# Routing a tile later and its row marks in two operations, expert blocks written out, expert sums in pairs of tiles

## The chip, the core and the metric

The kernel runs on one core of a Trainium2 chip. The metric is the device time of one execution in microseconds (us), as the median over runs; less is better. The five engines are named as in the profile: PE (matrix products; PEld is its weight load), DVE (vector), ACT (scalar activations), POOL (GpSimd, here mostly transfers by index) and SP (which starts the other transfers).

## What is computed

The input is 1024 rows (16 sequences of 64) of 256 numbers. Four layers are added to it in turn, each on a layer norm of the rows: an attention over a context, a mixture of eight experts, a second attention with rotated queries, and a second mixture of 32 masked experts of which each row takes one. The change touches the first mixture and what lies next to it:

```python
x = x + attention_0(layernorm(x), ctx, ctx)
# the first mixture, on h = layernorm(x):
logits = h @ router_w.T
top_w, top_i = top_k(softmax(logits), 2)            # two experts for each row
top_w = top_w / sum(top_w)
for e in range(8):
    gate, up = bitlinear(h, gate_w[e]), bitlinear(h, up_w[e])
    y_e = bitlinear(up * square(relu(gate)), down_w[e])
    out = out + combine[:, e:e + 1] * y_e
x = x + out
x = x + attention_1(layernorm(x), ctx, ...)
x = x + masked_experts(layernorm(x), ...)
# bitlinear(x, w) = quantised rows (scale 127 / max|row|) @ ternary weights (-1, 0, 1, times a mean).T
```

## The kernel before

The 1024 rows lie as eight tiles of 128 rows. Each engine has its own instruction stream, written out in order by hand, and the streams meet in semaphores.

**The first attention** goes over the eight tiles t. In the same passes ACT and DVE make the eight experts' weights ternary. DVE adds each tile's attention to X (`add_att`), measures the tile's mean and variance and hands it to POOL, which subtracts the mean (XC). At the pass t = 5 DVE also centres the router's weights (`r_raw`, three operations that wait for each other); at t = 7 PE turns them and ACT copies them to `rT`, in the middle of the tile's work. After the last tile DVE takes the largest value of each row (`row_peaks`), and PE makes the router's logits.

**Routing** places 2048 pairs of row and expert into 23 blocks (`NBLK`) of 128 rows, each block of one expert. `positions` works out the place of each pair and then marks, for each of 16 groups c of 128 pairs, the row of the block in a 128x128 table (`at_row`, 16 operations on DVE). PE's `sort` multiplies these marks with two tables for each group (which tile, which row of the tile): 32 matmuls into one sum, from which `owners` reads, with one conversion, which row of X belongs to each place of each block. POOL fetches the rows of a block by that list (`indirect_dma_start`, x_rows to xg).

**The expert blocks j = 0..22.** For each block: PE turns the fetched rows (`turn_rows`, L822), ACT copies them (L1311), PE makes gate and up (`gate_up`, L840), ACT makes relu (L1319), DVE multiplies relu by gate (L1747, below: gated) and by up (L1751), takes the largest magnitude of each row (L1755), from it the scales (L1726 to L1734, one number for each row), and the hidden rows are scaled and rounded: for even blocks by DVE (L1738), for odd blocks by ACT (L1333). PE turns the hidden rows (`turn_hidden`, L851), ACT copies them (L1323), PE makes the product with the third weight (`down`, L858), ACT scales the result (L1329), and POOL stores it by index (L602). In step j PE does `turn_hidden(j)`, `turn_rows(j+4)`, `gate_up(j+3)` and `down(j)` in this order. PE and DVE hold blocks 0 to 3 written out, then a loop of four blocks that is run `ROUNDS` = 4 times (on PE), and the rest written out; ACT's stream is written out. The expert of a block is read from a register that `run_of` loads, once for a turn of the loop, as seven experts in one word.

**Around the end of the blocks** PE folds the next attention's weights, eight units u (`fold_queries`, `fold_values`, `fold_keys`); units 0 and 1 are woven into the last three blocks. SP waits for the last stored block and loads the experts' results back (yg, four pairs of tiles). DVE adds them: for each tile two operations (L1824, L1825), each waiting for the one before, then the measure (L1840); after tiles 3 and 7 means and variances, POOL takes the roots, DVE makes the normed rows XN (L1818), PE turns them (L1060), ACT and DVE split them, and `project` (L981) starts the second attention. From there to the end PE's products set the pace.

Of the kernel before, what the change touches and what calls it, by code (L numbers as in the profile page):

```python
# [9 lines left out]
P = 128  # L10
NT = 8
# [101 lines left out]
def build(nc, x, ctx_in, cst_in, sel_in, kv_in, router_w, ffn_w, fold_in,  # L113
          weight_t, scale, masks_t, router_dt, out):
    with ExitStack() as ctx:
# [41 lines left out]
        iota_b = sb("iota_b", [P, P], BF16)  # L157
# [193 lines left out]
        raw_used, w_summed, w_total, w_rec_ready, hid_acted = (sem(n) for n in ("raw_used", "w_summed", "w_total", "w_rec_ready", "hid_acted"))  # L351
# [11 lines left out]
        h_scale_ready, relu_ready = sem("h_scale_ready"), sem("relu_ready")  # L363
# [51 lines left out]
        def positions(dve, link, R, start):  # L415
# [18 lines left out]
        def owners(dve, R, nth, B):  # L434
# [21 lines left out]
        def sort(pe, R, B, nth):  # L456

            n = R.choices * NT
            for c in range(n):
# [93 lines left out]
        def _(pool):  # L553
# [16 lines left out]
            pool.tensor_scalar(iota_b[:], cst[:, C_IOTA:C_IOTA + P], 1.0, 0.0, ALU.mult, ALU.add).then_inc(bconsts_built, 1)  # L570
# [77 lines left out]
        def _(pe):  # L648
# [115 lines left out]
            for t in range(NT):  # L764
# [9 lines left out]
                if t == NT - 1:  # L774
                    pe.wait_ge(r_centred, 1)
                    pe.wait_ge(w_rec_ready, NT)
                    for k in range(2):
                        mm = pe.transpose(bank[7][:, R_TURNED + k * NE:R_TURNED + (k + 1) * NE], r_raw[:, k * P:(k + 1) * P],
                                          identf[0:NE, 0:NE])
                    mm.then_inc(r_turned, 1)  # L780
# [8 lines left out]
                turn_probs(t, 3)  # L789
            turn_x1(2)  # L790
# [26 lines left out]
            def turn_rows(j, q, r):  # L817

                pe.wait_ge(gathered[r], 16 * q + 16)
# [12 lines left out]
            def in_run(word, k):  # L832
# [1290 lines left out]
```

## Time and profile before

| | us |
|---|---|
| median of 3 runs (444.98 to 446.79) | 445.58 |
| the profiled execution | 447.06 |
| its span, first to last instruction | 444.9 |
| PE busy | 371.3 |
| DVE busy | 329.6 |
| ACT busy | 212.3 |
| POOL busy | 142.9 |

The profiled execution is 1.5 us above the median of the runs; 2.2 us of it lie outside the span. Busy times are summed over the whole span, whose stages have different limits, so they don't say what a change in one stage is worth. The granted TensorE clock is a mean of 0.941 of full speed.

### The profile page before, as it was taken

Reading aid. Unit: us, or ns where it says so; the run is one execution under the profiler, and the core shown is the slowest. Engines: PE = TensorE matmul, PEld = TensorE weight load, DVE = VectorE, ACT = ScalarE, POOL = GpSimd, SP = SyncE. Lnnn points to the kernel's source line nnn. Section 1 sums busy time; section 2 is a strip of 40 time slices with the busy share of each in tenths; the row PEclk is TensorE's granted clock in tenths of the full one; section 3 lists DMA queues with packets and bytes.
Section 4 is the critical chain, followed back from the end, with each engine's and each line's share of the span. In section 5 each row is a group of like instructions: output and inputs, shape, how many; then the busy total and the mean of one; then the engine's idle time right before and its main releaser. Section 6 shows DMA issues by size and latency. Waiting matters only on the chain.

```text
span 444.9 us, 10555 instructions
## 1 busy us (share of the span) xinstructions
PE 371.3 (83%) x3670; PEld 257.3 (58%) x3677; DVE 329.6 (74%) x847; ACT 212.3 (48%) x466; POOL 142.9 (32%) x147
## 2 busy tenths in 40 slices
PE   2687877935877779989999999999999989538995
PEld 1466666922444446767457566466574778526884
DVE  6959999797888887798588778886875544673453
ACT  3699998552778887763013222231232221225441
POOL 1111211325466644020283142240440410153334
PEclk9999998955799999998999999999999999859999
DMA  8996760421365531540103112022031101343001
GB/s 271 405 411 224 296 246 4 173 66 36 85 213 165 178 136 49 176 159 14 66 30 96 43 55 96 2 95 96 1 97 55 41 1 70 121 113 89 19 32 38
DMA packets 17199, 50.77 MB, mean 114 GB/s; under 512 B 2120, under 2 KB 6480, under 8 KB 15104
## 3 DMA queue, kind: packets, MB, share of 16 engines
q1 hardware_dynamic: 14288, 42.46, 26.7%
q0 software_dynamic: 2864, 7.68, 5.8%
q8 instruction: 30, 0.49, 0.5%
q14 instruction: 17, 0.14, 0.1%
HBM read 43.44 MB, written 6.69 MB: 113 GB/s over the span
## 4 chain that ended last, share of the span: by engine, by line
PE 60%; DVE 14%; ACT 10%; issue 7%; DMA 6%; SPq 1%; POOL 1%; ACTq 0%; DVEq 0%; POOLq 0%
PE bank L981 17%; PE bank L1195 8%; PE bank L997 6%; PE bank L1069 5%; DMA raw<-in_L_ffn_w_dram 3%; PE bank L840 3%; PE bank L1008 3%; PE bank L851 3%; ACT W L1228 2%; PE bank L1022 2%; PE bank L858 2%; ACT hid L1333 2%; PE bank L1048 2%; PE bank L1032 2%; PE bank L710 1%
## 5 line engine op out<-in xcount | busy, mean ns | idle before, releaser
L1799 DVE TENSOR_TENSOR roped<-bank,cst 128x512 f32<-128x512 f32 x96 | 61.1, 685 | 29.4 <-PE bank L981 28.4
L623 POOL TENSOR_TENSOR WE<-WE,wT 128x512 f32<-128x512 f32 x32 | 42.3, 1348 | 82.0 <-DMA WE<-_L_ffn_expert_masks_dram 82.0
L981 PE MATMUL bank<-XNT_hi,AW_hi 128*128 128x512 f32 x96 | 42.2, 439 | 0.0
L1378 ACT ACTIVATE qrT<-bank 128x512 f32<-128x512 f32 x16 | 8.7, 595 | 62.3 <-PE bank L1008 62.3
L981 PE MATMUL bank<-XNT_lo,AW_hi 128*128 128x512 f32 x96 | 38.0, 396 | 0.0
L981 PE MATMUL bank<-XNT_hi,AW_lo 128*128 128x512 f32 x96 | 37.8, 394 | 0.0
L1372 ACT ACTIVATE prob<-prob 128x512 f32<-128x512 f32 x16 | 10.1, 632 | 44.3 <-DVE prob L1809 44.3
L997 PE MATMUL bank<-roped,MW 128*64 128x512 f32 x128 | 31.0, 605 | 0.0
L1069 PE MATMUL bank<-VW,ctxT 128*128 128x256 f32 x128 | 30.7, 385 | 0.0
L981 PEld LDWEIGHTS bank<-XNT_hi,AW_hi 128*128 128x128 f32 x96 | 18.2, 190 | 19.5 <-issue 11.4
L602 POOL DMA_INDIRECT y_rows<-y,slot x23 | 22.6, 983 | 20.7 <-ACT y L1329 18.3
L840 PE MATMUL bank<-W,xgT 128*128 x86 | 25.6, 423 | 3.0 <-ACT xgT L1311 2.6
L595 POOL DMA_INDIRECT xg<-x_rows,owner_b x23 | 22.4, 973 | 17.6 <-ACT hs L1314 11.0
L1228 ACT ACTIVATE W<-raw 128x1024 bf16<-128x1024 f32 x24 | 25.4, 1071 | 3.3 <-DMA raw<-in_L_ffn_w_dram 3.3
L576 POOL TENSOR_SCALAR XC<-X,mv 128x256 f32<-128x256 f32 x7 | 10.7, 1524 | 45.8 <-DVE mv L1620 45.8
L851 PE MATMUL bank<-identf,hid 128*128 128x128 f32 x92 | 15.3, 291 | 11.5 <-ACT hid L1333 7.1
L1069 PEld LDWEIGHTS bank<-VW,ctxT 128*128 128x128 f32 x128 | 23.2, 190 | 2.6
L710 PE MATMUL bank<-identf,pnat 128*128 128x128 f32 x128 | 21.8, 298 | 2.8 <-ACT pT L1220 2.8
L1747 DVE SCALAR_TENSOR_TENSOR hid<-bank,relu 128x512 f32<-128x512 f32 x23 | 15.9, 690 | 10.9 <-ACT relu L1319 10.8
L1195 PE MATMUL bank<-WE,pT_d 128*128 x80 | 21.4, 407 | 1.3 <-ACT pT_d L1457 0.7
L1500 DVE TENSOR_REDUCE mx<-bank 128x8 f32<-128x512 f32 x32 | 19.8, 681 | 1.9 <-PE bank L676 1.8
L1323 ACT ACTIVATE hidT<-bank,less_magic 128x512 bf16<-128x512 f32 x23 | 15.8, 687 | 10.7 <-PE bank L851 10.6
(313 smaller groups left out, 896.0 us busy)
## 6 DMA issues: line engine op xcount, KB each, us to landing
raw<-in_L_ffn_w_dram SPq DMA_DIRECT2D x8, 1536.0 KB, 8.1
fold<-in_L_xattn_fold_dram SPq DMA_DIRECT2D x8, 1024.0 KB, 6.6
WE<-_L_ffn_expert_masks_dram SPq DMA_DIRECT2D x8, 1024.0 KB, 5.3
kv<-in_keys_values_dram SPq DMA_DIRECT2D x8, 656.0 KB, 9.3
yg<-y_rows SPq DMA_DIRECT2D x8, 256.0 KB, 5.2
x_tok<-pay SPq DMA_DIRECT2D x8, 256.0 KB, 2.2
X<-in_x_dram SPq DMA_DIRECT2D x4, 256.0 KB, 10.1
x_rows<-xrow SPq DMA_DIRECT2D x2, 258.0 KB, 3.4
```

Source lines behind the costliest of these rows:

```text
L595: pool.indirect_dma_start(out=xg[j % 4][:].bitcast(U32), out_offset=None, in_=x_rows, in_offset=bass.IndirectOffsetOnAxis(ap=RB.owner[:, j ...
L602: pool.indirect_dma_start(out=y_rows, out_offset=bass.IndirectOffsetOnAxis(ap=slot[:, b:b + 1], axis=0), in_=y[b % 4][:], in_offset=None). ...
L623: pool.tensor_tensor(WE[:, e], WE[:, e], wT[:], ALU.mult).then_inc(WE_ready, 1)
L710: mm = pe.transpose(bank[4 + kvl % 2][:, c * P:(c + 1) * P], pnat[kvl][:, c * P:(c + 1) * P], identf[:])
L840: mm = pe.matmul(bank[2 + 2 * m - par][:], xgT[par][:, k * P:(k + 1) * P], W[:, bass.ds(e, 1), m, k * FF:(k + 1) * FF].rearrange("p a i -> ...
L851: mm = pe.transpose(bank[5][:, k * P:(k + 1) * P], hid[r][:, k * P:(k + 1) * P], identf[:])
L981: mm = pe.matmul(bank[g][:], a[:, k, c * P:(c + 1) * P], b[:, k, g * 512:(g + 1) * 512], start=k == 0 and i == 0, stop=k == 1 and i == 2)
L997: pe.matmul(bank[2 + g][half(h, g) * S:(half(h, g) + 1) * S, :], MW[u][:, r, at:at + S], roped[n][:, r, :], start=r == 0, stop=False, skip ...
L1069: mm = pe.matmul(bank[t % 4][:, 0:H], ctxT[:, u, t * P:(t + 1) * P], VW[:, u, :], start=u == 0, stop=u == NU - 1)
L1195: mm = pe.matmul(bank[4 + r % 4][:, 0:H], pT_d[r % 4][:, k * P:(k + 1) * P], WE_k[:, bass.ds(e, 1), k, :].rearrange("p a o -> p (a o)"), s ...
L1228: ins = act.activation(W[:, e, m, :], raw[e % 3][:, m, :], ACT.Abs, accum_out=w_sum[e % 2][:, m:m + 1])
L1799: ins = dve.tensor_tensor(roped[n][:, r, :].rearrange("p (b s) -> p b s", s=S), src, cst[:, None, at:at + S].to_broadcast([P, 8, S]), ALU. ...
```

## The change

Four parts:

1. The router's weights are centred at the pass t = 6 on DVE (was t = 5), turned by PE and copied by ACT after the passes (was in the middle of t = 7). `row_peaks` takes tiles 0 and 1 at t = 7, tile 2 later and 3 to 6 last (was 0, then 1, then 2 to 6).
2. The 16 marks become two operations of eight groups each. `sort` has one matmul of two tables (46 columns) for each group, and `owners` adds the two halves in two operations. POOL's `iota_b` goes.
3. The blocks are written out on PE and DVE. DVE scales every block's hidden rows, ACT none; ACT makes the output scale (one number for each row). `down` comes one step later: in step j PE does `turn_hidden(j)`, `turn_rows(j+4)`, `gate_up(j+3)` and `down(j-1)`; one `down` is left at the end. Two words of experts are loaded at the start, three more in steps 2, 6 and 10.
4. The experts' results are added in pairs of tiles, the first operation of both tiles ahead of the second of either. PE turns the first two pairs of XN after `fold_queries(7)` and ahead of `fold_values(7)` and `fold_keys(7)` (was after them).

```diff
@@ positions, owners (DVE), sort (PE)
-            dve.wait_ge(bconsts_built, 4)
-            for c in range(n):
-                dve.tensor_scalar(R.at_row[:, c], iota_b[:], lo[:, c:c + 1], None, ALU.is_equal).then_inc(spots_ready, 1)
+            for k in range(R.choices):
+                c = slice(k * NT, (k + 1) * NT)
+                dve.tensor_tensor(R.at_row[:, c], lo[:, c, None].to_broadcast([P, NT, P]),
+                                  cst[:, None, C_IOTA:C_IOTA + P].to_broadcast([P, NT, P]), ALU.is_equal).then_inc(spots_ready, 1)
...
-            dve.tensor_copy(R.owner[:], B[:, 0:R.n_blk]).then_inc(owner_ready, 1)
+            link(dve.tensor_copy(owner_tile[:], B[:, R.n_blk:2 * R.n_blk]))
+            dve.tensor_tensor(R.owner[:], owner_tile[:], B[:, 0:R.n_blk], ALU.add).then_inc(owner_ready, 1)
...
-                pe.wait_ge(spots_ready, c + 1)
-                for part in (1, 2):
-                    mm = pe.matmul(B[:, 0:R.n_blk], R.at_row[:, c, :], R.of_block[:, part, c, :],
-                                   start=c == 0 and part == 1, stop=c == n - 1 and part == 2)
+                pe.wait_ge(spots_ready, c // NT + 1)
+                mm = pe.matmul(B[:, 0:2 * R.n_blk].rearrange("p (a b) -> p a b", a=2), R.at_row[:, c, :], R.of_block[:, 1:3, c, :],
+                               start=c == 0, stop=c == n - 1)
@@ blocks, PE
-            with pe.Fori(0, ROUNDS) as i:
-                word = run_of(i)
-                for r in range(4):
-                    j = 4 * i + r
-                    e_up, e_down = in_run(word, r + 3), in_run(word, r)
-                    turn_hidden(r, 2 * i + r // 2)
-                    turn_rows(j + 4, i + 1, r)
-                    gate_up(j + 3, (r + 1) % 2, e_up)
-                    down(j, r % 2, e_down)
...
+            runs = [run_of(i) for i in range(2)]
+            for j in range(NBLK):
...
+                turn_hidden(j)
+                if j + 4 < NBLK:
+                    turn_rows(j + 4)
+                if j + 3 < NBLK:
+                    gate_up(j + 3, expert_at(j + 3))
+                if j:
+                    down(j - 1, expert_at(j - 1))
+                if j % 4 == 2 and len(runs) <= ROUNDS:
+                    runs.append(run_of(len(runs)))
...
+            down(NBLK - 1, expert_at(NBLK - 1))
...
             for u in range(2, NU):
                 fold_queries(u, 0)
                 fold_queries(u, 1)
+                if u == NU - 1:
...
+                    turn_x2(0)
+                    turn_x2(1)
                 fold_values(u)
                 fold_keys(u)
@@ blocks, ACT
-                if j % 2 == 0 and j + 1 < NBLK:
-                    scale_hidden(j + 1)
-                outputs(j)
+                output_scale(j)
+                if j:
+                    outputs(j - 1)
+            outputs(NBLK - 1)
@@ first attention, DVE
-                    row_peaks(0, 1)
+                    row_peaks(0, 2)
...
-                if t == NT - 3:
+                if t == NT - 2:
                     dve.wait_ge(r_loaded, 16)
...
-            row_peaks(2, NT - 1)
+            row_peaks(3, NT - 1)
@@ blocks, DVE (written out, one step)
+                if j:
+                    link.after(highest)
+                    scale = link.note(dve.tensor_scalar(was[:, 2:3], was[:, 1:2], was[:, 0:1], EPS, ALU.mult, ALU.max))
...
+                gated = link.note(dve.scalar_tensor_tensor(h[:], bank[2 - par][:], 0.0, relu[par][:], ALU.max, ALU.mult))
+                if j:
+                    link.after(scale)
+                    inverse = link.note(dve.reciprocal(was[:, 3:4], was[:, 2:3]))
+                link.after(gated)
+                dve.tensor_tensor(h[:], h[:], bank[4 - par][:], ALU.mult).then_inc(hid_done, 1)
+                if j:
+                    link.after(inverse)
+                    factor = link.note(dve.tensor_scalar(was[:, 4:5], was[:, 3:4], was[:, 0:1], QMAX, ALU.mult, ALU.mult))
+                dve.wait_ge(hid_done, j + 3)
+                highest = link.note(dve.tensor_reduce(hs[j % 4][:, 1:2], h[:], AX.X, ALU.max, apply_absolute_value=True))
+                if j:
+                    link.after(factor)
+                    dve.tensor_scalar(hid[(j - 1) % 4][:], hid[(j - 1) % 4][:], was[:, 4:5], MAGIC, ALU.mult, ALU.add).then_inc(hid_scaled, 1)
@@ sums, DVE
-            for t in range(NT):
-                add_experts(t)
-                link(dve.bn_stats(stats[:, t, :], X[:, t, :]))
-                if t == NT // 2 - 1:
-                    half_variances(0)
-            half_variances(1)
+            for c in range(NT // 2):
+                added = first_choices(c)
+                if c == 2:
+                    aggregated = half_means(0, measured)
+                second_choices(c, added)
+                if c == 2:
+                    half_variances(0, aggregated)
+                measured = measure(c)
+            half_variances(1, half_means(1, measured))
```

## Rows read from the trace of the kernel before

**Rows 1.** The page, the chain that ended last: shares of the span.

```profile
PE 60%; DVE 14%; ACT 10%; issue 7%; DMA 6%; SPq 1%; POOL 1%; ACTq 0%; DVEq 0%; POOLq 0%
```

**Rows 2.** Timeline, end of the first attention: start us, duration us, instruction [idle before <-releaser].

```profile
69.01 0.38 DVE L1623 BATCH_NORM_STATS2 r_stats<-r_raw 8x6 f32<-8x256 f32 x1
...
74.92 2.07 ACT L1214 ACTIVATE pnat<-bank 128x512 f32<-128x512 f32 x4 [0.44 <-PE bank L701]
...
79.64 0.36 DVE L1521 RECIPROCAL den_rec<-bank 128x32 f32<-128x32 f32 x1 [1.27 <-PE bank L732]
...
87.27 1.48 DVE L1515 TENSOR_REDUCE row_max<-XC 128x5 f32<-128x1280 f32 x1
```

**Rows 3.** Timeline, routing: marks, sort and owners.

```profile
95.92 3.28 DVE L432 TENSOR_SCALAR at_row_b<-iota_b,pos_b 128x128 bf16<-128x128 bf16 x16
...
97.09 2.40 PE L465 MATMUL bank<-of_block_b,at_row_b 128*128 128x23 bf16 x32 [4.32 <-DVE at_row_b L432]
...
99.52 0.18 DVE L437 CAST owner_b<-bank 128x23 uint32<-128x23 f32 x1
```

**Rows 4.** Tile at_row_d (second mixture): duration ns min/median/max, start.

```profile
L1949 DVE TENSOR_TENSOR at_row_d<-slot_lo,cst x1: 1219/1219/1219, 389.3 to 389.3; 128x1024 bf16<-128x1024 uint32 x1
```

**Rows 5.** Waits, 95 to 240 us: us in total, times, longest us.

```profile
DVE hid L1747 <- ACT relu L1319: 10.8, 17, 2.0
...
PE bank L851 <- ACT hid L1333: 7.1, 10, 0.8
...
PE bank L851 <- issue: 4.1, 4, 1.3
```

**Rows 6.** Timeline of PE: turn_hidden of blocks 1, 11 and 19.

```profile
117.07 0.66 PE L851 MATMUL bank<-identf,hid 128*128 128x128 f32 x4 [0.76 <-ACT hid L1333]
...
145.77 0.66 PE L851 MATMUL bank<-identf,hid 128*128 128x128 f32 x4 [0.69 <-ACT hid L1333]
...
168.75 0.65 PE L851 MATMUL bank<-identf,hid 128*128 128x128 f32 x4 [0.70 <-ACT hid L1333]
```

**Rows 7.** Timeline of DVE: block 13, and the next block's first operation.

```profile
145.08 0.68 DVE L1747 SCALAR_TENSOR_TENSOR hid<-bank,relu 128x512 f32<-128x512 f32 x1
...
145.80 0.68 DVE L1751 TENSOR_TENSOR hid<-hid,bank 128x512 f32<-128x512 f32 x1
...
146.72 0.68 DVE L1755 TENSOR_REDUCE hs<-hid 128x1 f32<-128x512 f32 x1
147.32 0.48 DVE L1738 TENSOR_SCALAR hid<-hid,hs 128x512 f32<-128x512 f32 x1
148.19 0.69 DVE L1747 SCALAR_TENSOR_TENSOR hid<-bank,relu 128x512 f32<-128x512 f32 x1 [0.40 <-ACT relu L1319]
```

**Rows 8.** Timeline of POOL in the blocks: one fetch.

```profile
145.15 0.97 POOL L595 DMA_INDIRECT xg<-x_rows,owner_b  x1 [0.31 <-issue]
```

**Rows 9.** Line L830, PE's register load of a word: ns min/median/max.

```profile
L830 PEldq TENSOR_LOAD <-run_e x5: 300/427/495, 111.0 to 159.6; - x5
```

**Rows 10.** Groups of instructions, 78 to 206 us: busy us, mean ns | idle.

```profile
L858 PE MATMUL bank<-W,hidT 128*128 x92 | 15.3, 283 | 1.2 <-ACT hidT L1323 0.2
```

**Rows 11.** Timeline, from the returned expert results to the second attention.

```profile
188.94 0.49 DVE L1824 SCALAR_TENSOR_TENSOR X<-yg,gate,X 128x256 f32<-128x256 f32 x1 [0.49 <-DMA yg<-y_rows]
...
189.98 0.43 DVE L1840 BATCH_NORM_STATS2 stats<-X 128x6 f32<-128x256 f32 x1
190.44 0.48 DVE L1824 SCALAR_TENSOR_TENSOR X<-yg,gate,X 128x256 f32<-128x256 f32 x1
...
196.57 0.65 PE L888 MATMUL bank<-fold 128*64 128x256 f32 x4
...
198.94 2.84 DVE L1818 TENSOR_SCALAR XN<-X,mv,rstd 128x256 f32<-128x256 f32 x8
...
199.82 1.21 PE L1060 MATMUL bank<-identf,XN 128*128 128x128 f32 x8 [1.79 <-DVE XN L1818]
...
203.03 0.79 PE L981 MATMUL bank<-XNT_hi,AW_hi 128*128 128x512 f32 x1
```

More of the change, by code:

```diff
@@ L773, in _ @@
                     turn_queries(t + 2)
[L774 to L780, printed above, removed]
                 if t:
@@ L789, in _ @@
                 turn_probs(t, 3)
+            pe.wait_ge(r_centred, 1)
+            pe.wait_ge(w_rec_ready, NT)
+            for k in range(2):
+                mm = pe.transpose(bank[7][:, R_TURNED + k * NE:R_TURNED + (k + 1) * NE], r_raw[:, k * P:(k + 1) * P], identf[0:NE, 0:NE])
+            mm.then_inc(r_turned, 1)
             turn_x1(2)
@@ L830, in run_of, with expert_at, gate_up @@
                 return pe.value_load(run_e[0:1, bass.ds(i, 1)], min_val=0, max_val=(1 << 3 * RUN) - 1)
-            def in_run(word, k):
-                return (word >> (3 * k)) & (NE - 1)
-            def gate_up(j, par, e):
+            def expert_at(j):
+                i = min(j // 4, ROUNDS)
+                return (runs[i] >> (3 * (j - 4 * i))) & (NE - 1)
+            def gate_up(j, e):
+                par = j % 2
                 pe.wait_ge(xgT_ready, j + 2)
@@ L1630, in _ @@
             measured = link.note(dve.bn_stats(stats[:, NT - 1, :], X[:, NT - 1, :]))
-            row_peaks(1, 2)
+            row_peaks(2, 3)
             link.after(measured)
@@ L1736, in scale_even @@
-            def scale_even(j, r):
-                dve.wait_ge(h_scale_ready, j + 1)
-                dve.tensor_scalar(hid[r][:], hid[r][:], hs[r][:, 4:5], MAGIC, ALU.mult, ALU.add).then_inc(hid_scaled, 1)
-            def hidden(j, r):
-                par = r % 2
-                first = isinstance(j, int) and j == 0
-                if not isinstance(j, int) or j >= 4:
+            for j in range(NBLK):
+                h, par = hid[j % 4], j % 2
+                was = hs[(j - 1) % 4]
+                if j:
+                    link.after(highest)
+                    scale = link.note(dve.tensor_scalar(was[:, 2:3], was[:, 1:2], was[:, 0:1], EPS, ALU.mult, ALU.max))
+                if j >= 4:
@@ L1745, in hidden @@
                     dve.wait_ge(h_turned, j - 1)
                 dve.wait_ge(relu_ready, j + 1)
-                gated = link.note(dve.scalar_tensor_tensor(hid[r][:], bank[2 - par][:], 0.0, relu[par][:], ALU.max, ALU.mult))
-                if not first:
-                    scale = row_scale((r + 3) % 4)
+                gated = link.note(dve.scalar_tensor_tensor(h[:], bank[2 - par][:], 0.0, relu[par][:], ALU.max, ALU.mult))
+                if j:
+                    link.after(scale)
+                    inverse = link.note(dve.reciprocal(was[:, 3:4], was[:, 2:3]))
@@ L1754, in hidden @@
                 dve.wait_ge(hid_done, j + 3)
-                link.note(dve.tensor_reduce(hs[r][:, 1:2], hid[r][:], AX.X, ALU.max, apply_absolute_value=True))
-                if r % 2:
-                    scale_even(j - 1, r - 1)
-            for j in range(4):
-                hidden(j, j)
-            with dve.Fori(1, ROUNDS + 1) as i:
-                link.enter(i - 1, 16)
-                for r in range(4):
-                    hidden(4 * i + r, r)
-                link.leave(ROUNDS, 16)
```

138 lines of the change are left out of this document (64 added, 74 removed).

## The prediction

> **What bounds the kernel now.** I read the chain that ended last first, to see which engine's time is the kernel's time and where it changes hands. Over the span it is mostly PE's, with a few per cent of "issue", time in which an engine waited for nothing that the profile shows [rows 1]. The change lies in the stretches where the chain leaves PE, so I read those in their own timelines. In the end of the first attention and in routing the chain runs through DVE, operation after operation, each waiting for the one before. In the expert blocks I read the waits and then the starts of `turn_hidden`: block 1 at 117.07, block 19 at 168.75 [rows 6], 51.68 us for 18 blocks, 2.87 a block. No engine fills that. DVE idles 10.8 us for ACT's relu. PE waits 7.1 us in ten blocks for the odd blocks' hidden rows, which ACT scales, and 4.1 us in four places as "issue" [rows 5]; those four, 3.9 to 4.0 blocks apart, are the turns of the written loop and its exit. After the blocks DVE has the chain, from the returned results to the first XN [rows 11]. From `project` on PE is full, and nothing there hangs on a fixed time: SP's and POOL's transfers wait for semaphores of the same stretch. So what is won before 203.03 arrives at the end.
>
> **Part 1, centring a tile later.** At t = 5 three dependent DVE operations start at 69.01, the first 0.38 long, so together at most 1.1 [rows 2], ahead of the maxima for tile 7. The exponentials of tile 7 start at 74.92, and ACT had idled 0.44 before them for PE, which had waited for those maxima [rows 2]. So at most 0.44 comes back; then ACT is late next. At t = 6 the three operations meet cover: before 79.64 DVE idles 1.27 for PE [rows 2], and 1.1 fits in; without that idle they would cost up to 1.1 again, and the gain would be lost. PE's two small turns and ACT's copy go past the last tile's turns; they were in the stream before and stay in it, so I count them at nothing, with 0.3 as the bound for the loss. The last `row_peaks` takes four tiles instead of five: 1.48/5 is 0.30 less [rows 2], the fifth being measured at t = 7 while DVE waits anyway. Sum: 0.7 won, between 0.0 and 1.2.
>
> **Part 2, marks.** Now 16 marks run from 95.92 for 3.28; PE's 32 small matmuls follow them, first start 97.09, 2.40 long, and end 0.3 behind the last mark; the conversion ends at 99.70 [rows 3]. The new operation stands in the trace in the second mixture: 128x1024 from two broadcast inputs took 1.219 [rows 4]. Two of them, overlapping by 0.08 as neighbours on DVE do (146.72 to 147.32 is 0.60 for a 0.68 operation [rows 7]), end at 95.92+1.14+1.22 = 98.28. PE can do the first eight groups meanwhile. The second eight I take at 0.5 (0.075 a matmul is the pitch now, 2.40/32, itself held back by the marks; with twice the columns between 0.04 and 0.10 each, so 0.3 to 0.8). Then two dependent operations for `owners`, 0.18 and 0.2 with a wait between, instead of one 0.18: end near 99.25, 0.45 earlier, bounds 0.15 and 0.65. The extra add for `slot` is covered, since POOL wants it only at its ninth fetch.
>
> **Part 3, the blocks.** DVE's step after the change, from rows of block 13 [rows 7]: gated to up 0.72 (145.08 to 145.80, one small operation between, as after); up to the largest magnitude is 0.92 now with three small operations between, one afterwards, so 0.73; largest magnitude to scaling 0.60; scaling 0.48, of which 0.08 overlaps, and a small operation (0.72-0.60 = 0.12) to the next gated: 0.52. Together 2.57 a block. The same count for the step before gives 2.44 a block, and its idle 10.8/23 = 0.47 makes 2.91, which is about the 2.87 measured, so the count is sound. The other loop that could set the pace: scaled rows to `turn_hidden`, to `gate_up(j+3)`, relu, to gated of block j+3. From 145.77 to 148.19 that is 2.42 [rows 6, 7], 2.47 with the hand-over, and it may take 2x2.57 less the 2.53 from gated to the end of scaling, 2.61. So DVE sets the pace by 0.14. ACT loses a 128x512 operation every second block and gains one of a single number a block, so it has more room than before. POOL needs a fetch and a store a block, 2x(0.97+0.31) = 2.56 [rows 8]: as much as DVE, but its fetches run four blocks ahead, which hides its jitter.
> PE's register loads stay: each takes 0.43 [rows 9] and about 0.2 of unpacking, now in steps 2, 6 and 10 behind `down`. PE's own work in a block is 2.87 less its waits, (7.1+4.1)/18 [rows 5]: 2.25 of a 2.57 step, so 0.32 of a load's 0.6 shows, less the 0.14 of slack: some 0.2 each at least, 0.6 at most; I take 0.5 for the three, near the lower end, because the whole loads of the loop now, three branches and four loads together, show as 4.1. 18 blocks: 18x2.57+0.5 = 46.8 against 51.68, 4.9 won. At the start PE idles 0.76 before block 1 for ACT's scaling [rows 6]; DVE has that scaling done earlier, and `down(0)` no longer stands ahead: 0.7 won. At the end one `down` more stands behind the last blocks, where PE also folds and is full: 15.3/23 = 0.67 [rows 10], of which I take 0.6 lost. Sum: 5.0 won. Bounds: 1.8 (pace 2.75) and 5.9 (loads free, end free).
>
> **Part 4, sums in pairs.** From the second pair's arrival to the first XN it takes 198.94-188.94 = 10.0. A tile takes 1.50 (188.94 to 190.44: two sums of 0.52, each waiting for the other, and a measure of 0.46) [rows 11]; in pairs each operation is two away from the one it needs, so it starts when the engine is free: 0.41, 0.41 and 0.35 for a tile, 1.17. Six tiles: 2.0 less, and XN starts 2.0 earlier. That neighbours without a wait do overlap is seen in the eight XN, 2.84/8 = 0.355 each.
> The Trainium skill (VectorE: DVE Perf Modes, "The DRAIN you can't avoid") says that the next operation does not start until the pipe is empty, so that taking semaphores out between operations saves nothing; by it this part would win nothing on DVE, and the whole change 2.0 less.
> The rows of block 13 and of XN differ from that rule by 0.06 to 0.12 an operation, and I go by them.
> PE does not get all of the 2.0. It idled 1.79 before its first turn, and fold 7's last part, 196.57 to 198.03, 1.46 long, lay ahead of that idle [rows 11]. Now the first XN pair is there at 197.8; two turns with the second pair's wait end at 199.1; then comes the fold's 1.46, to 200.6; the last two turns, whose rows have been there since 199.9, take 1.2: `project` at 201.8 instead of 203.03. 1.2 won; bounds 2.0, and a loss of 0.8 if DVE saves nothing and the fold then stands on the path. ACT's later copies of unit 7 follow PE's turns as before.
>
> **Sum.** 0.7+0.45+5.0+1.2 = 7.35 off the profiled execution's 447.06: 439.7. That execution stands 1.5 above the median of the runs, so against the median 445.58 I expect 438.2.
>
> **Rivals.**
> *The pace of the blocks is set higher.* DVE and POOL now both need 2.56 a block, with nothing spare on DVE. If hand-overs add 0.18, the pace is 2.75 and part 3 wins 1.8: 441.4. For it: two engines at the limit. Against: DVE's order has every small operation's input ready before it. 0.15.
> *The pairs win nothing, and the fold gets in the way*: part 4 loses 0.8, 440.2. For it: the turns of pairs 2 and 3 stand behind 1.46 of other work. Against: 0.52 against 0.40 for the same operation. 0.12.
> The Trainium skill's rule named in part 4 would give this case.
> *Parts 1 and 2 arrive nowhere*, because POOL's first fetch also waits until the quantised rows are stored: 439.4. Against: the profile puts POOL's wait down to the list that `owners` writes, not to the store. 0.07.
> *Slower*: PE's stream, written out, runs late at every block as it does now at the loop's turns, where "issue" takes 1.0 on average [rows 5]. The pace is then above 2.87 instead of below. At 2.87 part 3 is gone (443.1); for slower by 0.5% it needs about 3.1, 0.53 of PE standing still beyond what DVE's pace hides; at 3.2 it gives 449. Against: blocks 16 to 22 are written out already, and block 19 waits for ACT's scaling, not for "issue" [rows 6]. 0.05.
>
> **How the numbers follow.** My forecast has 0.61. A measurement of this kernel can tell about 0.5%, 2.2 us, from no change. Faster means below 443.4: the forecast, the pairs' case and the third rival lie there whole, the pace rival by three quarters: 0.90 at most; I say 0.88. Same: the rest of the pace rival and mixtures, 0.08. Slower 0.04. The upper end: the pace rival with one other part failing, 442.6. The lower: part 1 at 1.2, part 3 at 5.9 and part 4 at 2.0 with part 2 at 0.65 is 9.75, 435.8, and 435.5 is the end I take.
>
> **What would show it.** `turn_hidden` of blocks 1 to 19 should span about 47 us, at a pace near 2.6; PE's "issue" of 4.1 and its waits for ACT should be gone from L851, and DVE's wait for relu should shrink to 1 or 2 us. If DVE still idles for relu, the PE loop sets the pace. The two marks should take 2.4, the first XN should come about 8 us after the second pair's arrival, and PE should go from fold 7 into `project` with less than 1 us idle. The prediction is wrong if the pace is above 2.75, or if PE stands between the turns of XN.

## The result, and the profile after

The changed kernel takes 439.71 us (median of 4 runs, 439.28 to 442.13); the kernel before took 445.28 beside it (4 runs). The ratio is 0.9889, with a 95% interval of 0.9851 to 0.9927: 5.6 us less, where 7.4 had been forecast; 438.2 against 439.7. In the two profiled executions, which the sum was made against, it is 447.06 against 439.53, 7.5 less where the sum said 7.35. That agreement is luck: three of the four terms of the sum were off by about 1 each, the stretch behind them, taken as fixed, gave 2.7 back, 1.4 came from where these two executions started, and all that cancels.

In the chain of the changed kernel DVE, ACT and "issue" have smaller shares than before [rows 1]:

```profile
PE 49%; DVE 7%; DMA 2%; issue 2%; ACT 1%; POOL 0%; SPq 0%; DVEq 0%; ACTq 0%
```

These shares add up to 61% of the span, so they only say where to look. I then lined up the two timelines at events that both have. Each line is a stretch of the path, its length before and after, and what was won:

| stretch | before | after | won |
|---|---|---|---|
| start to the addition of tile 4's attention to X | 65.73 | 64.31 | 1.42 |
| to the marks of the experts, `hot_b` (part 1) | 25.52 | 23.63 | 1.89 |
| to the end of the list of owners (part 2) | 8.45 | 8.96 | -0.51 |
| to block 1's `turn_hidden` (part 3, start) | 17.37 | 15.73 | 1.64 |
| to block 19's `turn_hidden` (steady state) | 51.68 | 46.90 | 4.78 |
| to the last `down` (tail) | 9.20 | 10.21 | -1.01 |
| to the arrival of the second pair of results | 10.99 | 11.57 | -0.58 |
| to the first XN (part 4) | 10.00 | 7.68 | 2.32 |
| to the first turn of probabilities | 37.49 | 37.23 | 0.26 |
| to the sixth such turn | 88.43 | 89.92 | -1.49 |
| to the first turn of the finished rows | 37.62 | 38.58 | -0.96 |
| to the end of the span | 82.42 | 82.68 | -0.26 |

The gains of the first nine lines come to 10.2; the full stretch of PE, which the prediction took as fixed, gives 2.7 back. Nothing of the change lies on the path to the first line's event, which came anywhere from 64.2 to 67.2 in the 14 profiles of this study. So 1.4 of the 7.5 is where these two executions happened to start from.

**The blocks.** Timeline of PE (start, duration, instruction, idle before and its releaser), and the waits of PE and DVE (us, times, longest):

```profile
112.63 1.02 PE L851 MATMUL bank<-identf,hid 128*128 128x128 f32 x4
116.00 0.66 PE L851 MATMUL bank<-identf,hid 128*128 128x128 f32 x4 [0.94 <-DVE hid L1746]
...
159.53 0.66 PE L851 MATMUL bank<-identf,hid 128*128 128x128 f32 x4 [0.49 <-DVE hid L1746]
169.74 0.65 PE L859 MATMUL bank<-W,hidT 128*128 x4 [0.81 <-ACT y L1328]
```

```profile
PE bank L851 <- DVE hid L1746: 9.5, 19, 0.9
PE bank L859 <- ACT y L1328: 0.8, 1, 0.8
DVE hid L1733 <- ACT relu L1317: 3.3, 4, 1.8
```

PE's waits for ACT's hidden rows (7.1) and the four "issue" gaps (4.1) of [rows 5] are gone. PE now waits 0.49 for DVE at each turn, and DVE, which had idled 10.8 for relu, does so four times, at the start (3.3, where 1 or 2 were expected). DVE's own rows give the pace: from one gated to the next 2.56 us with no idle time; 2.57 was forecast from [rows 7].

```profile
118.54 0.68 DVE L1733 SCALAR_TENSOR_TENSOR hid<-bank,relu 128x512 f32<-128x512 f32 x1
119.14 0.15 DVE L1736 RECIPROCAL hs<-hs 128x1 f32<-128x1 f32 x1
119.26 0.69 DVE L1738 TENSOR_TENSOR hid<-hid,bank 128x512 f32<-128x512 f32 x1
119.86 0.21 DVE L1741 TENSOR_SCALAR hs<-hs 128x1 f32<-128x1 f32 x1
119.99 0.68 DVE L1743 TENSOR_REDUCE hs<-hid 128x1 f32<-128x512 f32 x1
120.58 0.48 DVE L1746 TENSOR_SCALAR hid<-hid,hs 128x512 f32<-128x512 f32 x1
120.97 0.21 DVE L1729 TENSOR_SCALAR hs<-hs 128x1 f32<-128x1 f32 x1
121.10 0.68 DVE L1733 SCALAR_TENSOR_TENSOR hid<-bank,relu 128x512 f32<-128x512 f32 x1
```

**Routing**, the surprise. Timeline of DVE, POOL and PE:

```profile
92.61 2.65 DVE L432 TENSOR_TENSOR at_row_b<-pos_b,cst 128x1024 bf16<-128x1024 f32 x2
95.18 0.64 DVE L1690 TENSOR_TENSOR below<-counts_b,cst 128x184 f32<-128x184 f32 x1
96.72 0.18 DVE L439 TENSOR_TENSOR owner_b<-owner_tile,bank 128x23 uint32<-128x23 f32 x1
...
92.77 2.84 POOL L586 TENSOR_TENSOR of_block_b<-of_block_b,cst 128x184 bf16<-128x184 bf16 x2 [3.24 <-DVE of_block_b L428]
...
95.67 0.80 PE L467 MATMUL bank<-of_block_b,at_row_b 128*128 128x46 bf16 x16 [6.20 <-POOL of_block_b L586]
```

PE did not start on the first eight marks while the second eight were made. It waited for POOL's two small multiplications (`of_tile`), which end at 95.61. They are not part of the diff, and the forecast did not look at them. POOL's first fetch starts 0.91 behind the end of the list here and before, so what routing wins or loses does arrive.

### The profile page after: what moved, and what is told of

It reads as the page before. It is cut to its first block, busy times and chain, and to the rows that moved or that the text cites. A ratio compares the mean times of both kernels' runs of the same rounds, so it can differ in the third digit from the quotient of the medians.

```text
span 437.4 us, 10370 instructions
## 1 busy us (share of the span) xinstructions
PE 365.2 (83%) x3660; PEld 254.1 (58%) x3660; DVE 328.1 (75%) x823; ACT 207.3 (47%) x478; POOL 146.0 (33%) x146
## 3 DMA queue, kind: packets, MB, share of 16 engines
q0 software_dynamic: 2864, 7.68, 6.0%
## 4 chain that ended last, share of the span: by engine, by line
PE 49%; DVE 7%; DMA 2%; issue 2%; ACT 1%; POOL 0%; SPq 0%; DVEq 0%; ACTq 0%
PE bank L989 17%; PE bank L1194 9%; PE bank L1005 6%; PE bank L1068 6%; PE bank L1016 3%; PE bank L1030 2%; PE bank L1056 2%; PE bank L1040 2%; DMA yg<-y_rows 1%; DVE prob L1796 1%; PE bank L1096 1%; DVE X L1805 1%; DVE s_stat L1794 1%; DMA y_rows<-y,slot 1%; DVE X L1812 1%
## 5 line engine op out<-in xcount | busy, mean ns | idle before, releaser
L1068 PE MATMUL bank<-VW,ctxT 128*128 128x256 f32 x128 | 32.2, 399 | 0.0
L1372 ACT ACTIVATE prob<-prob 128x512 f32<-128x512 f32 x16 | 10.1, 631 | 45.6 <-DVE prob L1790 45.6
L842 PE MATMUL bank<-W,xgT 128*128 x92 | 27.1, 422 | 2.2 <-ACT xgT L1309 2.2
L1068 PEld LDWEIGHTS bank<-VW,ctxT 128*128 128x128 f32 x128 | 24.2, 198 | 3.0
L711 PE MATMUL bank<-identf,pnat 128*128 128x128 f32 x128 | 20.6, 284 | 2.5 <-ACT pT L1219 2.5
L989 PEld LDWEIGHTS bank<-XNT_hi,AW_lo 128*128 128x128 f32 x96 | 18.1, 189 | 4.3
```

Source lines behind the costliest of these rows:

```text
L711: mm = pe.transpose(bank[4 + kvl % 2][:, c * P:(c + 1) * P], pnat[kvl][:, c * P:(c + 1) * P], identf[:])
L842: mm = pe.matmul(bank[2 + 2 * m - par][:], xgT[par][:, k * P:(k + 1) * P], W[:, bass.ds(e, 1), m, k * FF:(k + 1) * FF].rearrange("p a i -> ...
L989: mm = pe.matmul(bank[g][:], a[:, k, c * P:(c + 1) * P], b[:, k, g * 512:(g + 1) * 512], start=k == 0 and i == 0, stop=k == 1 and i == 2)
L1068: mm = pe.matmul(bank[t % 4][:, 0:H], ctxT[:, u, t * P:(t + 1) * P], VW[:, u, :], start=u == 0, stop=u == NU - 1)
```

## The experiments

**Each part undone, in turn.** Four kernels: the changed kernel with the diff of one part reversed and the other three kept; of each diff the core is shown. They ran five rounds on one chip, beside 17 runs of the kernel before, median 444.79. The changed kernel ran beside other runs of it, first with a median of 445.28, later with one of 445.69; so a difference of 1 us between these groups is not shown by the times.

Part 1 undone:

```diff
-                if t == NT - 2:
+                if t == NT - 3:
                     dve.wait_ge(r_loaded, 16)
...
-            row_peaks(3, NT - 1)
+            row_peaks(2, NT - 1)
```

> The changed kernel with part 1 undone: the router's rows centred at t = 5 again, their turns back inside the last tile, five tiles in the last maxima. The prediction priced part 1 at 0.7, so 440.4 beside 439.7 for the changed kernel. Theory A, from the events of the two profiles (events came 1.42 earlier before the part and 3.30 earlier at the first MAX8 behind it): 1.9, so 441.6. In the profile: by theory A the exponentials of tile 7 come some 0.5 later and the reciprocals behind them, with DVE idle ahead of them again, some 1.2 later than in the changed kernel, counted from the same start of the last additions; by the prediction together 0.7.

440.19 us, ratio 0.9896 (0.9861 to 0.993), 0.5 more than the changed kernel's first median, 1.4 more than its second (below). In the profile the stretch is 25.52 again, 1.89 more. Of this, 0.54 is that the exponentials of tile 7 come later, a little over the cap of 0.44 that the forecast had read; 0.63 is added between them and the reciprocals, where PE's clock is lower; 0.27 is the last maxima (1.48 for five tiles, 1.21 for four); the other 0.44 falls between the last two tiles and was not taken apart. Timeline and stretches of PE without part 1 (of a stretch: start:end, length, busy time and number of matmuls, granted clock as a share of 2.4 GHz, DMA share, GB/s):

```profile
76.44 1.83 PE L726 MATMUL bank<-pT,kv 128*18 128x64 f32 x64
```
```profile
77.00:79.00 2.00, 2.00 (x52) 0.50 0.02 4
```

and of the changed kernel:

```profile
73.48 1.09 PE L726 MATMUL bank<-pT,kv 128*18 128x64 f32 x64
```
```profile
73.00:75.00 2.00, 2.00 (x72) 1.00 0.06 16
```

Without part 1 PE idles 0.80 for the maxima of tile 7, which stand behind the centring, and 0.57 for their turned copy, and then runs the 64 matmuls of `weigh` at 1.2 GHz, 0.74 slower. With part 1 only the 0.57 is left, and the clock stays up. Of the 14 profiles of the study, the two without part 1 show 1.8 to 1.9 there and the twelve with it 1.09. In seven of those twelve the maxima at the end of the stretch then wait 0.4 to 0.9 for ACT's logits: the router's last 16 matmuls take 3.1 to 3.4 there and 1.85 in the changed kernel's profile, and the clock is lower (0.50 at 84:86 in the repeat, 1.00 in the first profile). So part 1 brings 0.9 to 1.9 in all.

Part 2 undone:

```diff
-            for k in range(R.choices):
-                c = slice(k * NT, (k + 1) * NT)
...
+            for c in range(n):
+                dve.tensor_scalar(R.at_row[:, c], iota_b[:], lo[:, c:c + 1], None, ALU.is_equal).then_inc(spots_ready, 1)
...
+                for part in (1, 2):
+                    mm = pe.matmul(B[:, 0:R.n_blk], R.at_row[:, c, :], R.of_block[:, part, c, :],
```

> The changed kernel with part 2 undone: sixteen marks from bf16 and 32 matmuls of 23 columns again. The prediction priced part 2 at 0.45 won, so 440.15. Theory A: the part loses 0.5, because POOL's two multiplications for the blocks' tiles, which run beside DVE's marks, take 1.4 each beside the new marks where they took 0.5 beside the old ones, and PE's matmuls wait for them; so 439.2, and in the profile POOL's two take about 0.95 together again, and the list of owners is there about 0.5 sooner after the marks' start. Rival B: POOL's two are slow in the changed kernel for another reason (a transfer, ACT's copy beside them); then they stay near 2.8 here.

436.91 us, ratio 0.9815 (0.9776 to 0.9855): without part 2 the median is lower, by 2.8 against the changed kernel's first and by 1.9 against its second; the intervals of the ratios touch, so the events have to decide. Theory A holds for routing, and routing is the smaller half:

```profile
94.98 3.28 DVE L432 TENSOR_SCALAR at_row_b<-iota_b,pos_b 128x128 bf16<-128x128 bf16 x16
98.58 0.18 DVE L437 CAST owner_b<-bank 128x23 uint32<-128x23 f32 x1
...
95.15 0.95 POOL L585 TENSOR_TENSOR of_block_b<-of_block_b,cst 128x184 bf16<-128x184 bf16 x2 [3.25 <-DVE of_block_b L428]
```

From the marks' start to the final operation of the list is 3.60 here and 4.11 with part 2. Another 1.5 lies a hundred microseconds later (from the first to the sixth turn of probabilities 88.43 here, 89.92 with part 2); see the placement and the pause below.

Part 3 undone:

```diff
-            for j in range(NBLK):
...
+            with pe.Fori(0, ROUNDS) as i:
...
+                    down(j, r % 2, e_down)
...
+                if j % 2 == 0 and j + 1 < NBLK:
+                    scale_hidden(j + 1)
+                outputs(j)
```

> The changed kernel with part 3 undone: the written loop, ACT scaling the odd blocks, down a step earlier. Prediction: 5.0 lost, 444.7. Theory A, by events: 1.7 at the start, 4.8 for 18 blocks, 1.0 given back at the end, 5.4: 445.1, with turn_hidden of blocks 1 to 19 at 51 to 52 us again. Rival C: a part of the 5.4 is given back behind the blocks whatever part 3 does (the later stretch of the changed kernel is 2 to 3 us longer than before in the profiles); then less, 442 to 443.

442.27 us, ratio 0.9936 (0.9904 to 0.9968): 2.6 more than the changed kernel's first median, 3.5 more than its second (below). By events theory A is right: `turn_hidden` of blocks 1 to 19 takes 51.61, and from the first turned rows to the last `down` 74.29 instead of 69.07, 5.2 more. Rival C is right about the time: this kernel lacks a pause that costs the changed kernel 1.2 in PE's full stretch. In its profile the results also come back 1.0 sooner behind the last `down` (10.53 against 11.57), which is no part of the diff.

Part 4 undone:

```diff
-            for c in range(NT // 2):
-                added = first_choices(c)
...
+            for t in range(NT):
+                add_experts(t)
+                link(dve.bn_stats(stats[:, t, :], X[:, t, :]))
```

> The changed kernel with part 4 undone: sums tile by tile, all four turns of XN behind the folds. Prediction: 1.2 lost, 440.9. Theory A, by events (2.3 from the second pair's arrival to XN, 2.7 at the first scores): 442.3. Rival C: what is won before PE's full stretch is given back in it: no difference. Rival by the Trainium skill's rule that overlapping operations on DVE saves nothing (VectorE: DVE Perf Modes, The DRAIN you can't avoid): from the second pair's arrival to XN no more than in the changed kernel, 7.7, against 10.0 by theory A.

441.12 us, ratio 0.9921 (0.9891 to 0.9951), 1.4 to 2.4 more than the changed kernel. From DVE's first sum of the second pair (181.00, which had no wait in this execution) to the first XN (191.01) it takes 10.01 again:

```profile
181.00 0.49 DVE L1799 SCALAR_TENSOR_TENSOR X<-yg,gate,X 128x256 f32<-128x256 f32 x1
181.52 0.48 DVE L1800 SCALAR_TENSOR_TENSOR X<-yg,gate,X 128x256 f32<-128x256 f32 x1
182.04 0.43 DVE L1815 BATCH_NORM_STATS2 stats<-X 128x6 f32<-128x256 f32 x1
```

With part 4 two first sums take 0.80 together:

```profile
181.31 0.88 DVE L1805 SCALAR_TENSOR_TENSOR X<-yg,gate,X 128x256 f32<-128x256 f32 x2 [1.81 <-DMA yg<-y_rows]
182.11 0.88 DVE L1812 SCALAR_TENSOR_TENSOR X<-yg,gate,X 128x256 f32<-128x256 f32 x2
182.90 0.75 DVE L1818 BATCH_NORM_STATS2 stats<-X 128x6 f32<-128x256 f32 x2
...
188.99 2.84 DVE L1799 TENSOR_SCALAR XN<-X,mv,rstd 128x256 f32<-128x256 f32 x8
```

That is 0.52 an operation where each waits for the one before, and 0.40 where it doesn't. The Trainium skill (VectorE: DVE Perf Modes, "The DRAIN you can't avoid") says that taking the semaphores out between operations on DVE saves nothing; that does not describe these rows. The same section adds that a next operation that is not held starts earlier, and with that the rows agree; the prediction left this out.

**The turns of XN.** The pairs kept, PE's order undone:

```diff
-                if u == NU - 1:
...
-                    turn_x2(0)
-                    turn_x2(1)
...
-            turn_x2(2)
-            turn_x2(3)
+            for h in range(NT // 2):
+                pe.wait_ge(XN_ready, h + 1)
...
```

> The changed kernel, with the sums in pairs but all four turns of XN behind the last fold again. The prediction gave PE's new order a price, 0.8 of DVE's 2.0, for the fold in front of the last turns: without it project would start up to 0.8 sooner after XN, or, if the order helps, later. In the profiles XN to project takes 4.27 in the changed kernel and 4.09 with part 4 undone; theory G: the order of the turns is worth nothing, 4.1 here, since PE is through the fold before XN arrives. Rival: 4.9 and more, the fold being ahead of the first turn then.

One run, 438.01. XN to `project` took 4.62, between theory G and the rival, but this execution does not tell them apart: the load of fold 7 came late, and PE idled for it.

```profile
187.84 1.57 PE L879 MATMUL bank<-fold 128*128 128x192 f32 x8 [1.08 <-DMA fold<-in_L_xattn_fold_dram]
```

So the fold was still running when XN arrived at 188.78. What the order is worth with the load in time stays open.

**Where the buffers lie.** In PE's full stretch a unit takes 17.68 before the change, 17.75 after it, and 17.68 without part 2. Part 2 replaces a buffer of 256 bytes a partition by one of 92, which takes 96, and everything allocated behind it moves by 160 bytes.

```diff
-        owner_tile = sb("owner_tile", [P, NBLK])
+        owner_tile = sb("owner_tile", [P, 64])[:, 0:NBLK]
```

> The changed kernel, with owner_tile allocated at 256 bytes a partition instead of 96, so that every later buffer lies where it lay before the change; no instruction differs. In the full stretch of PE a unit takes 17.75 in the changed kernel and 17.68 before it; undoing parts 1, 3 or 4 leaves 17.75, undoing part 2 gives 17.68. Theory D: the addresses of the buffers make the 0.07 (a 128x512 matmul of project every 0.2335 instead of 0.2316); then 17.68 or 17.69 here, some 0.45 less over the units. Rival E: it comes with part 2's instructions; then 17.75. The pause of 0.9 to 1.3 inside the context matmuls before the sixth turn of the probabilities, at the same instruction in the changed kernel and with parts 1 or 4 undone, stays by a theory F that it belongs to a place in PE's stream (27 of 32 matmuls, then the pause); by the rival that it is chance or comes of addresses it goes.

One run, 436.0 us. Timelines of PE, second and third turn of probabilities, with the edit:

```profile
242.99 1.03 PE L1040 MATMUL bank<-identf,prob 128*128 128x128 f32 x8
...
260.68 1.03 PE L1040 MATMUL bank<-identf,prob 128*128 128x128 f32 x8
```

17.69. Theory D holds for this pair of kernels: no instruction differs, and a matmul of `project` follows the other after 0.231 on average instead of 0.233. One profile doesn't fit: the shift run below has the old addresses too and takes 17.73 (0.232), so the addresses are not the only thing that counts. Over the study the five other kernels with the old addresses have 17.68 or 17.69, the eight with the new ones 17.74 to 17.76.

And the pause stayed:

```profile
299.85 0.63 PE L1056 MATMUL bank<-probT,kvr 64*64 64x64 f32 x27
301.48 0.34 PE L1056 MATMUL bank<-probT,kvr 64*64 64x64 f32 x5 [1.00 <-issue]
```

as in the changed kernel:

```profile
301.03 0.63 PE L1056 MATMUL bank<-probT,kvr 64*64 64x64 f32 x27
302.54 0.34 PE L1056 MATMUL bank<-probT,kvr 64*64 64x64 f32 x5 [0.89 <-issue]
```

**The pause.** The last edit adds eight matmuls to PE's stream at a place where PE waits for DVE anyway:

```diff
-            for t in range(NT):
+            for t in [*range(NT), *range(NT)]:
```

> The pad run's kernel with PE's eight turns of the keys and values, ahead of routing, done twice (the same result again), while PE waits for DVE there anyway. Eight matmuls more stand ahead of everything that follows. Theory F, the pause belongs to a place in PE's stream: it comes eight matmuls earlier, after 19 of the 32 context matmuls and not after 27, about as long as before. Rival: it belongs to those instructions or to what else happens at that time; then it stays after 27. If it is gone, its place is one where PE waits anyway.

One run, 435.92. The pause is gone, from that place and from the rest of the full stretch:

```profile
299.74 0.65 PE L1056 MATMUL bank<-probT,kvr 64*64 64x64 f32 x32
300.20 0.65 PE L1030 MATMUL bank<-kvrT,qrT 64*64 64x64 f32 x32
300.67 0.65 PE L1056 MATMUL bank<-probT,kvr 64*64 64x64 f32 x32
```

It did not move by eight, so theory F was wrong on where it would go. What the profiles do show is that it goes with PE's program: nine of the 14 have as many matmuls written ahead of that point as the changed kernel, and all pause after matmul 27 of 32, for 0.9 to 1.25, whatever differs on other engines and in addresses; the five with another number (before, parts 2 and 3 undone, this one, and the first combination below) don't pause in that stretch.

The traces hold more on this: each load of instructions is a transfer of its own kind. The larger ones, 16 KB each, go by this queue (of the changed kernel; packets, MB, share):

```profile
q8 instruction: 32, 0.52, 0.5%
```

I set their starts beside the fifth turn of probabilities. In the nine profiles with the pause such a load starts 3.1 to 3.2 us behind that turn, PE stops 1.2 to 1.4 later, and it goes on 2.2 to 2.5 behind the load's start. In the five without, the load starts 1.9 to 2.1 us ahead of that turn, 5 us earlier; so in the shift run too. In all 14 the load before it starts 13.0 to 13.6 us ahead. So the pause goes with a late load of instructions, 14 times out of 14. That PE waits for this very load, and why it comes late, is argued from this and was not shown by an edit.

**The tiles on DVE.** POOL's two multiplications go between DVE's two marks:

```diff
+                if R.choices == 2 and k == 0:
+                    dve.wait_ge(of_block_ready, 1)
+                    for m in range(2):
+                        cm = slice(m * NT, (m + 1) * NT)
+                        ins = dve.tensor_tensor(R.of_block[:, 1, cm], R.of_block[:, 0, cm],
+                                                cst[:, C_TILE:C_TILE + NT, None].to_broadcast([P, NT, NBLK]), ALU.mult)
+                    ins.then_inc(of_tile_ready, 1)
...
-            pool.wait_ge(of_block_ready, 1)
...
-            ins.then_inc(of_tile_ready, 1)
```

> The changed kernel, with the blocks' two multiplications for the tiles on DVE, between the two marks, and not on POOL beside them. Theory A (POOL is slow because DVE's new marks run beside it): the two take about 0.25 each on DVE, PE's matmuls start right behind them, and from the marks' start to the list of owners it takes 3.6 or less instead of 4.11. Rival: PE's matmuls with 46 columns are what is late; then 4.1 stays.

One run, 437.03. 3.67 from the marks to the list:

```profile
93.54 1.22 DVE L432 TENSOR_TENSOR at_row_b<-pos_b,cst 128x1024 bf16<-128x1024 f32 x1
94.67 0.60 DVE L438 TENSOR_TENSOR of_block_b<-of_block_b,cst 128x184 bf16<-128x184 bf16 x2
95.19 1.22 DVE L432 TENSOR_TENSOR at_row_b<-pos_b,cst 128x1024 bf16<-128x1024 f32 x1
97.21 0.18 DVE L446 TENSOR_TENSOR owner_b<-owner_tile,bank 128x23 uint32<-128x23 f32 x1
...
95.33 0.49 PE L474 MATMUL bank<-of_block_b,at_row_b 128*128 128x46 bf16 x8 [4.94 <-DVE of_block_b L438]
96.47 0.49 PE L474 MATMUL bank<-of_block_b,at_row_b 128*128 128x46 bf16 x8 [0.64 <-DVE at_row_b L432]
```

PE now does its first eight while DVE makes the second eight marks, as the forecast had supposed. So part 2, cured of the wait, is no better than the 16 marks: 3.67 against 3.60, in one profile each.

**The tail.** In the changed kernel the last `down` idles 0.81 for ACT's copy of block 21, which stands behind the first fold's high part and a scale. The edit puts the copy first:

```diff
                 hidden_rows(j, j % 2)
-                if j >= NBLK - 2:
-                    high_part(0, j - NBLK + 2)
+                if j == NBLK - 2:
+                    high_part(0, 0)
...
+                if j == NBLK - 1:
+                    outputs(j - 1)
+                    high_part(0, 1)
                 output_scale(j)
-                if j:
+                if 0 < j < NBLK - 1:
                     outputs(j - 1)
```

> The changed kernel, with ACT's last block in another order: the copy of block 21's output directly behind block 22's hidden rows, and the high part of the first fold and block 22's scale behind it. Theory: in the changed kernel the last down idles 0.81 for that copy, which stands behind those two; here it idles 0.2 or less, the last output is there 0.6 sooner, and from turn_hidden of block 19 to the last down it takes 9.6 instead of 10.21. Rival: the wait moves to the fold, whose next operation waits for the high part; then the last down still comes 10.0 or more after block 19.

One run, 437.16. From block 19 (159.01) to the last `down` 9.65:

```profile
168.66 0.65 PE L859 MATMUL bank<-W,hidT 128*128 x4 [0.25 <-ACT y L1328]
```

0.56 of the 1.01 lost in the tail was this wait. What remains, 0.45, I put down to the `down` that now stands later; no run took that apart.

**Repeat and combinations**, five rounds each on one chip, beside 11 runs of the kernel before, median 445.69.

> The changed kernel itself, so that it stands beside the two combinations on one chip. 439 to 440, as in its first runs. In its profile the parts of the path that hang on no clock and no transfer should repeat to 0.05: 4.67 from the first mark of the experts to the marks, 4.11 from the marks to the owners, 17.75 a unit; the pause before the sixth turn of the probabilities should be there again, 0.9 to 1.3.

438.77 us (437.41 to 440.23), ratio 0.983 (0.9782 to 0.9879), 6.9 less than the kernel before beside it; the stretches repeat (4.68, 4.10, 17.75) and so does the pause, 0.89.

> The changed kernel without part 2, and with ACT's last block in the order of the tail run. Undoing part 2 gave back 0.5 in routing, 0.45 over the units and, its stream being another, the pause of 1.0; the tail 0.56. Sum 2.5 below the changed kernel: 437.2 against 439.7. If the pause comes with ACT's order or by chance, 438.2.

436.18 us, ratio 0.9774 (0.972 to 0.9828), 2.6 below the changed kernel as expected; no pause. From block 19 to the last `down` it takes 9.64, so the tail's edit brings its 0.56 here too.

> The changed kernel with the three repairs together: owner_tile at 256 bytes (0.45), the tiles on DVE between the marks (0.44), ACT's last block in the other order (0.56). Sum 1.45 below the changed kernel: 438.2 against 439.7, with the pause in PE's stream still there. By the rival that the late clock and the transfers decide, no difference from the changed kernel that these runs can show.

437.23 us, ratio 0.9806 (0.9757 to 0.9856), 1.5 below the changed kernel, with the pause (1.00). The lowest median of these three has the changed kernel without its part 2, with ACT's last block reordered. The intervals of the three ratios overlap; it is the events in the profiles that carry the order between them. The shift edit was not combined with the others.

## Why the prediction was right, point by point

Both medians of the changed kernel, 439.71 and 438.77, lie in the stated range. The mechanism of part 3, which is most of the sum, was right; parts 1, 2 and 4 were not what was forecast, and their errors cancel with what happened behind them.

- *Part 1, 0.7 forecast, 0.9 to 1.9 measured.* The cap of 0.44 on the exponentials was nearly right (0.54), and so were the 0.30 for the maxima (0.27). Missed: PE's idle time there had cost twice, once as waiting and again as 64 matmuls at 1.2 GHz. The idle 1.27 of DVE before the reciprocals was partly that slow `weigh`, and not only room for the three moved operations.
- *Part 2, 0.45 won forecast, 0.51 lost measured.* The failed step is "PE can do the first eight groups meanwhile": they also need POOL's tiles. The new marks were read from a stretch in which POOL did nothing beside them [rows 4]; here POOL's two operations of 0.5 end 0.35 behind the end of each mark, 94.18 and 95.61, and the second mark and the `below` behind it take 0.3 longer than elsewhere (1.52 against 1.22, 0.64 against 0.34). So each engine stands while the other works. The Trainium skill states this (SBUF — State Buffer, "SBUF: two separate sides"): DVE and GpSimd have a pair of ports that one of them holds for a whole instruction, DVE with two inputs from SBUF among the cases. The rows agree: 0.95 for POOL's two beside marks with one tensor input, 2.84 beside marks with two. The new marks are also longer than the old ones; another stretch of the same trace speaks for the inputs and against the length, tiles `WE` and `AW_lo` (duration ns min/median/max):

```profile
L624 POOL TENSOR_TENSOR WE<-WE,wT x32: 1264/1290/1889, 217.1 to 341.5; 128x512 f32<-128x512 f32 x32
L1771 DVE TENSOR_TENSOR AW_lo<-AW_full,AW_hi x5: 947/949/951, 229.9 to 300.9; 128x768 fp32r<-128x768 f32 x5
```

Five of the 32 on POOL start beside an `AW_lo`, whose two inputs both lie in SBUF; these five take 1.78 to 1.89 and end 1.12 to 1.15 behind its end. The other 27 take 1.26 to 1.30, though DVE's operations of 0.69 with one input from SBUF work beside most of them. In one case POOL is the first: `prob<-prob,s_stat` on DVE, again with two inputs from SBUF, then takes 1.16; the other 15 times it takes 0.69. I had the rule at hand and did not ask who else ran beside the new form.
- *Part 3, 5.0 forecast, 5.4 measured* (1.64 + 4.78 - 1.01). The pace was right to 0.01, and the three register loads cost nothing that shows. The start was worth 1.64, not 0.7. The tail cost 1.01 instead of 0.6: 0.45 is left for the `down`, and the missing term is ACT's copy behind the fold's high part, 0.56 by the tail run.
- *Part 4, 1.2 forecast, 2.3 measured.* The 0.26 of the next line of the table is not part 4's: with part 4 undone XN to the first turn of probabilities takes 37.24, with it 37.23. DVE's 2.0 was nearly right (2.32); of the 0.8 that PE was to give back, 0.18 came (XN to `project` 4.27 against 4.09), and by the first turn of probabilities nothing is left of it. PE does not stand between the turns of XN, but still idles 1.64 ahead of the first. With part 4 undone PE's turns of XN run at 1.2 GHz behind its idle 1.78 and take 3.33; in the changed kernel the clock stays up, and the turns take less than I had read from [rows 11]. The stretch of PE with these turns, first without part 4 and then in the changed kernel:

```profile
194.00:196.00 2.00, 2.00 (x8) 0.50 0.00 0
```
```profile
192.00:194.00 2.00, 2.00 (x21) 1.00 0.00 0
```

The fourth figure is the clock. That the order of the turns does this was not shown by itself, since the run on the order alone had the late load, and its clock stayed up as well.

- *"From `project` on PE is full, and nothing there hangs on a fixed time"* is the sentence that failed most dearly. PE stays full, but 0.07 a unit went to the new addresses, 1.2 to the pause in its stream, and 1.0 or more to the clock at 351:357, which was lower in five of the 14 profiles, with and without parts 2 and 3. PE waits 1.20 there for ACT in each of them and in the others; eight matmuls then take 3.18 here and 1.97 in the pad run. In the changed kernel:

```profile
351.28 0.63 PE L1131 MATMUL bank<-rdT,ones 128*128 128x32 f32 x4 [1.20 <-ACT ctxT L1389]
351.75 3.18 PE L1068 MATMUL bank<-VW,ctxT 128*128 128x256 f32 x8
```

None of the four rivals happened: the pace is 2.56, the pairs win 2.3 on DVE, what routing wins or loses arrives, and PE's stream is not late in the blocks. Why five rounds of one kernel spread over 3 to 5 us is now partly visible: the start (64.2 to 67.2), this clock (1.0), the return of the results (10.1 to 11.6), and the clock at the first blocks (the step from block 1 to 2 is 3.37 in the changed kernel, 2.56 in the tail run, where it had risen before 111 and not after 113).

## What to carry to other kernels

Before an operation's form is changed, list what the other engines run at that moment: a cheaper DVE operation with two tensor inputs made two small POOL operations three times as long, and PE waited for those. Price an idle gap of PE with the slow matmuls behind it, and line up two profiles stretch by stretch before believing a sum that came out right. When the allocation changes, look at whether later buffers moved: here 160 bytes went with 0.07 us a unit.

## What the runs showed of the hardware

- POOL's 128x184 bf16 multiplication takes 0.49 beside DVE marks with one tensor input and 1.41 or 1.47 beside those with two, and the next mark takes 1.52 instead of 1.22.
- The same matmuls, 128x512 f32, follow each other after 0.231 us on average, or 0.233 with the buffers 160 bytes lower (pad run); one kernel with the old addresses has 0.232.
- PE pauses 0.9 to 1.25 at one place of its stream, in the nine profiles with as many matmuls written ahead; in these a 16 KB load of instructions starts 2.2 to 2.5 before PE goes on, in the five others it starts 5 us earlier. Eight repeated matmuls ahead removed the pause in one run.
- After a gap of PE of 0.6 to 1.8 us the granted clock was found at 0.50 in some stretches behind it (77:79 behind 0.80 and 0.57, 194:196 behind 1.78) and at 1.00 in others (192:194, behind 1.64).
